# The first chunk of a two-FFN-and-attention kernel: seven up products lead its gates, the weight pieces are split in another order, and some small low parts move

## The chip, the cores and the metric

One core of a Trainium2 chip runs the whole program. The metric is device time in microseconds (us), from the start to the end of one execution. TensorE is called PE, VectorE DVE, ScalarE ACT, GpSimd POOL and SyncE SP, as in the profile; the SP engine issues most of the transfers.

## The reference

The input x has 2048 rows of 128 numbers. Three steps follow each other, each with a residual: half an FFN, attention, and the same half FFN again.

```
def ffn(x):                       # x: 2048 x 128, layer-normed
    shared = silu(x @ Ws_up) @ Ws_down              # 128 -> 64 -> 128
    aff = x @ centroids.T                           # 64 experts
    idx = top 8 of (aff + expert_biases)
    w = sigmoid(aff[idx]); w = w / (sum(w) + 1e-8)
    h = silu(x @ W_up[e]) for each of 64 experts    # 128 -> 64
    routed = sum_e cw[:, e] * (h_e @ W_down[e])     # cw: w scattered to 64 columns
    return shared + routed
x = x + 0.5 * ffn(layernorm(x))
x = x + softmax(q k^T) / sqrt(128) @ v              # q, k, v of layernorm(x)
x = x + 0.5 * ffn(layernorm(x))
```

All arrays are float32. All 64 experts are computed for every row, and the gates (cw) of the unchosen ones are zero.

## The kernel before, in words

**Chunks and units.** The rows are worked in chunks of 512 columns (the rows lie on the free axis, transposed). A chunk of the FFN has 33 units: unit 0 is the shared expert (64 partitions), and units 1 to 32 are pairs of experts (2 x 64 = 128 partitions). The FFN before the attention has chunks n = 0 to 3, that behind it n = 4 to 7. `U` is a unit's number counted over all chunks.

**Two parts for each product.** Every float32 operand of a product is split in a high part, rounded to float32r, and a low part, the rest. A product is then three matmuls: high by low, low by high, high by high (`product`, and the three lines of `down`, L1093 to L1095).

**One unit.** `up` (PE, L1055 to L1057) writes the hidden bank `hid[U % 4]`, one of four banks of PSUM. `silu_unit` (ACT, L430) applies silu. `gate_unit` (DVE, L672) multiplies by the gate row. `hi_unit` (ACT, L441) rounds the high part. `low_part` (L276) subtracts it, on DVE or, where `on_pool` says so, on POOL; in that case the gated value lies in one of three SBUF buffers `gated`, and else it lies in the hidden bank again. `down` (PE) adds the unit to `yacc`, four units behind `up`. `up` of unit U waits until bank U % 4 is free of unit U-4.

**Gates.** For units 7 to 32 a gate row comes by a transfer from DRAM, to which ACT's copy `gates` (L475) goes. For the units 1 to 6 of chunks 0 and 4 ("early" units) PE spreads the gate rows instead: `spread_gate` (L1080) multiplies the transposed weights `cwT` (ACT, L472) by a selection matrix, into one of two banks, so that unit u's spread waits for unit u-2's gate. Silu of an early unit writes into the SBUF buffer `wide`, and its gated value goes to the hidden bank.

**The order of the work** is written out by hand: each engine has its own program, with semaphores between them, and each works strictly in the order of its program. In the loop over units further steps hang on unit numbers: the prologue of the next chunk (its statistics, `normed` at units 5 and 6, PE's turn `pro_xT` at unit 8, L1134; `joint_product` at 11, `joint_turn` at 13, L1110, which waits for ACT's `joint_aff`, L450; the gate weights of the next chunk, POOL L374 and PE L1156 at 24).

**The first chunk's start.** ACT and DVE norm x, PE turns it (`first_xT`) and makes the affinities (`first_aff`); DVE picks the top 8 (`first_top`, `first_chosen`) and makes the weights (`first_weights`: L831, L832, L833). Meanwhile PE does `LEADS[0]` up products ahead, and `stay_awake` (L1223) matmuls whose result nobody reads. Then `pro_cw` (L1127) turns the weights, ACT copies them, and the loop over units begins. `LEADS` is (units of chunk 0, units of chunk 4).

**The weights.** W_up and W_down come in 8 pieces each of 128x512 numbers, into 14 buffers `raw`; even pieces are of W_up, odd ones of W_down, and one piece serves four units. `piece_hi` (ACT, L510) rounds a piece and `piece_lo` (POOL, L363) makes its low part. The first `PRE` pieces are split before the loop of chunk 0 and one more at each even unit. The semaphore `s_w` counts the split ones. `small` holds the small weights (centroids, Ws_up, Wv), `wsdn` the shared down weight, and `wsdn_pad` a padded copy that the shared expert of the chunks behind the first uses (`joint_down`). DVE's `small_lo` (L899) and `pad_lo` (L894) make their low parts; both subtract one SBUF tensor from another.

Of the kernel before, what the change touches and what calls it, by code (L numbers as in the profile page):

```python
# [35 lines left out]
PRE = 3  # L36
FIRST = 12
LEADS = (4, 2)
# [7 lines left out]
def macaron_kernel(nc, x_d, wup_d, wdn_d, wsup_d, wsdn_d, cent_d, bias_d, wq_d, wk_d, wv_d, gates_d, out_d):  # L46
# [21 lines left out]
    with ExitStack() as ctx:  # L68
# [178 lines left out]
        def on_pool(U):  # L247

            u, n = unit_at(U)
            if n == 0 and u < 25:  # L250
                return u > EARLY and u % 2 == 1
            return u == 15 or u % 3 != 0 and (u < UNITS - 1 or n % NCH < NCH - 1)
# [33 lines left out]
        def piece(k, part):  # L286

            w = (wup[part], flat(wdn[part]))[k % 2]
            return w[:, (k // 2) * PW:(k // 2 + 1) * PW]
# [4 lines left out]
        def _(sp):  # L294
# [8 lines left out]
            def load_piece(k):  # L303
                if k >= NR:
                    sp.wait_ge(s_w, k - NR + 1)
                src = (wup_d, wdn_d)[k % 2][:, (k // 2) * PW:(k // 2 + 1) * PW]
                sp.dma_start(raw[:, k % NR, :], src).then_inc(s_raw[k % NR], 16)

            for k in range(FIRST):
                load_piece(k)  # L310
                if k == 5:
                    load_x(1)
# [107 lines left out]
        def _(act):  # L420
            def silu_unit(u, n):
                U = place(u, n)
                m = P if u else F
                act.wait_ge(s_hid, U + 1)
                dst = hid[U % NH]
                if early_unit(u, n):
                    if nth_gated(u, n) > NB:
                        act.wait_ge(s_gated, nth_gated(u, n) - NB)
                    dst = wide[:, slot_of(u, n), :]
                nc.scalar.activation(dst[0:m, :], hid[U % NH][0:m, :], ACT.Silu).then_inc(s_silu, 1)  # L430
# [102 lines left out]
            for f in range(2):  # L533
                for c in range(NCH):
                    n = f * NCH + c
                    if c == 0:
                        if f == 0:
                            first_hi(0)
                            first_hi(1)
                            piece_hi(0)  # L540
                            act.wait_ge(s_value, 16 * 3)
                            nc.scalar.copy(small[0][:, E + F:LOADED], raws[:, E + F:LOADED]).then_inc(s_wh, 1)
                            nc.scalar.copy(wsdn[0][:, :], rawd[:, :]).then_inc(s_wh, 1)
                            act.wait_ge(s_spread, 1)
                            make_sel()
                            act.wait_ge(f_bias, 1)
                            nc.scalar.activation(flat(sil), bank[0][:, 0:TPC * E], ACT.Sigmoid).then_inc(p_sil, 1)
                            nc.scalar.activation(eps[:, 3:4], eps[:, 0:1], ACT.Silu)
                            piece_hi(1)
                            silu_unit(0, n)  # L550
                            silu_unit(1, n)
                            hi_unit(0, n)
                            silu_unit(2, n)
                            piece_hi(2)
                            pro_cwT(n)
                            silu_unit(3, n)
                    for u in range(min(c, 1), UNITS):
# [4 lines left out]
                        if n == 0 and u % 2 == 0 and PRE + u // 2 < 2 * WP:  # L562
                            piece_hi(PRE + u // 2)
                        if c + 1 < NCH:
                            if u == 9:
                                pro_hi(n + 1)
                            if u == 12:
                                joint_aff(n + 1)
                            if u == 13:
                                joint_silu(n + 1)  # L570
                            if u == 14:
                                joint_hi(n + 1)
                            if u == 16:
                                pro_sil(n + 1)
                            if u == 25:
                                pro_cwT(n + 1)
# [72 lines left out]
        def _(dve):  # L649
# [8 lines left out]
            def gate_unit(u, n):  # L658
# [3 lines left out]
                dve.wait_ge(s_silu, U + 1)  # L662
# [162 lines left out]
            def first_weights(n):  # L825
# [3 lines left out]
                inv = wsum[:, 1, :].unsqueeze(2).to_broadcast([P, TPC, E])  # L829
# [5 lines left out]
            def pro_sum(n):  # L835
# [4 lines left out]
                nc.vector.reciprocal(wsum[:, 1, :], wsum[:, 0, :]).then_inc(p_inv, 1)  # L840
# [45 lines left out]
            for f in range(2):  # L886
                for c in range(NCH):
                    n = f * NCH + c
                    if c == 0:
                        if f == 0:  # L890
# [18 lines left out]
                            small_lo(1, small, raws, E + F, LOADED)  # L909
                            small_lo(2, wsdn, rawd, 0, D)  # L910
                            lo_unit(0, n)
                            pad_lo()
                    for u in range(min(c, 1), UNITS):
# [3 lines left out]
                        if c + 1 < NCH:  # L917
                            if u == min(c, 1):
# [3 lines left out]
                            if u == 2:  # L922
                                stats(0, c + 1, p_st, (2, 3))
# [21 lines left out]
                        if c:  # L945
                            if u == 9:
                                epi_x(n - 1, c - 1)
                            if f == 0:
# [10 lines left out]
                                if u == 32:  # L959
                                    epi_proj_lo(c - 1)  # L960
                        if n == 0 and u == 14:
# [90 lines left out]
        def _(pe):  # L1052
# [6 lines left out]
            def up(u, n):  # L1059
                U = place(u, n)  # L1060
                if n == 0 and u and (u - 1) % (PAIRS // WP) == 0:
                    pe.wait_ge(s_w, 2 * ((u - 1) // (PAIRS // WP)) + 1)
                if U >= NH:
# [18 lines left out]
            def down(u, n):  # L1082
                U = place(u, n)
                m = P if u else F
                if n == 0 and u and (u - 1) % (PAIRS // WP) == 0:
                    pe.wait_ge(s_w, 2 * ((u - 1) // (PAIRS // WP)) + 2)
                if U == 0:
                    pe.wait_ge(s_wl, 3)
# [139 lines left out]
            for f in range(2):  # L1228
                for c in range(NCH):
                    n = f * NCH + c  # L1230
                    if n == 0:
# [5 lines left out]
                        stay_awake(2)  # L1237
# [167 lines left out]
```

## Time and profile before

| what | us |
|---|---|
| median of 3 runs (549.23 to 549.7) | 549.29 |
| the profiled execution | 549.5 |
| its span, first to last instruction | 547.7 |
| PE matmul busy | 533.3 (97%) |
| DVE / ACT / POOL busy | 408.5 / 412.2 / 274.6 |

The profile has one execution. The span is 1.8 us shorter than the time of the same execution. The program has no stage in which an engine other than PE is busy all the time for long; what is to be seen of the first chunk is where PE has gaps, and which engine's work ends last ahead of each.

### The profile page before, as it was taken

The page shows a single profiled execution, that of the slowest core. Times are in us where ns is not written, and L with a number is a line of the kernel's source. Part 1 is how long each engine was busy: PE and PEld are TensorE (multiplying, and loading weights), DVE is VectorE, ACT ScalarE, POOL GpSimd, SP SyncE. Part 2 cuts the span into 40 slices and gives each one's busy share as a digit, 9 for nine tenths or more (in the row PEclk, how much of TensorE's full clock was granted, in tenths as well). Part 3 has the DMA queues.
Part 4 walks back from the last instruction along what each step waited for, and adds up shares of the span by engine and source line. Part 5 has one row for each costly group of instructions (what it writes and reads, how often), then busy time and mean ns, then how long its engine had stood idle before and what let it go on. Part 6 is the DMA issues. An engine that isn't in the chain of part 4 may idle for free.

```text
span 547.7 us, 8638 instructions
## 1 busy us (share of the span) xinstructions
PE 533.3 (97%) x2683; PEld 436.2 (80%) x2683; DVE 408.5 (75%) x926; ACT 412.2 (75%) x814; POOL 274.6 (50%) x242
## 2 busy tenths in 40 slices
PE   8899999999999999899999998999999999999997
PEld 6677887887888886699999998877888888788885
DVE  5979679777966676667777888778677867966664
ACT  7899878877887775666666666678788777878774
POOL 3579767775866773000000000066675766766763
PEclk9999999999999999999999999999999999999999
DMA  8676554554565540000000000055565565656652
GB/s 259 189 203 198 182 193 164 178 194 154 173 187 181 187 156 1 1 1 1 1 2 0 2 1 1 11 183 162 176 197 174 177 185 178 175 170 193 198 192 95
DMA packets 44271, 72.25 MB, mean 132 GB/s; under 512 B 8865, under 2 KB 9633, under 8 KB 44225
## 3 DMA queue, kind: packets, MB, share of 16 engines
q1 hardware_dynamic: 43568, 71.17, 41.7%
q8 instruction: 21, 0.34, 0.3%
q10 hardware_dynamic: 592, 0.39, 0.2%
q0 software_dynamic: 64, 0.13, 0.1%
q14 instruction: 26, 0.20, 0.1%
HBM read 69.57 MB, written 2.10 MB: 131 GB/s over the span
## 4 chain that ended last, share of the span: by engine, by line
PE 87%; DVE 6%; ACT 3%; issue 2%; POOL 1%; POOLq 0%; DVEq 0%
PE lrow L1055 13%; PE lrow L1056 12%; PE lrow L1057 12%; PE bank L1093 10%; PE bank L1095 10%; PE bank L1094 10%; PE bank L1127 6%; PE bank L1327 3%; PE bank L1329 3%; PE bank L1328 3%; PE bank L1223 1%; POOL gpart_lo L276 1%; ACT gpart_hi L441 1%; DVE pmax L873 1%; PE bank L1134 1%
## 5 line engine op out<-in xcount | busy, mean ns | idle before, releaser
L276 POOL TENSOR_TENSOR gpart_lo<-gated,gpart_hi 128x512 fp32r<-128x512 f32 x174 | 224.5, 1296 | 168.3 <-ACT gpart_hi L441 163.9
L430 ACT ACTIVATE lrow<-lrow 128x512 f32<-128x512 f32 (+1 forms) x246 | 143.6, 584 | 64.7 <-PE lrow L1057 64.3
L672 DVE TENSOR_TENSOR gated<-lrow,wide 128x512 f32<-128x512 f32 x170 | 116.5, 685 | 51.2 <-ACT lrow L430 47.5
L441 ACT CAST gpart_hi<-gated 128x512 fp32r<-128x512 f32 x174 | 106.9, 614 | 2.9 <-DVE gated L672 2.5
L1093 PE MATMUL bank<-gpart_lo,wdn_hi 128*128 128x512 f32 x256 | 101.4, 396 | 1.0 <-POOL gpart_lo L276 1.0
L1095 PE MATMUL bank<-gpart_hi,wdn_hi 128*128 128x512 f32 x256 | 101.5, 396 | 0.0
L1094 PE MATMUL bank<-gpart_hi,wdn_lo 128*128 128x512 f32 x256 | 100.8, 394 | 0.0
L672 DVE TENSOR_TENSOR lrow<-lrow,wide 128x512 f32<-128x512 f32 x74 | 51.5, 697 | 34.9 <-ACT lrow L430 34.7
L990 DVE TENSOR_TENSOR pT_lo<-bank,pT_hi 128x512 fp32r<-128x512 f32 x64 | 43.7, 685 | 25.7 <-ACT pT_hi L616 25.7
L1093 PEld LDWEIGHTS bank<-gpart_lo,wdn_hi 128*128 128x128 f32 x256 | 48.0, 188 | 13.5 <-POOL gpart_lo L276 1.9
L276 DVE TENSOR_TENSOR gpart_lo<-lrow,gpart_hi 128x512 fp32r<-128x512 f32 (+1 forms) x84 | 57.3, 683 | 1.0 <-ACT gpart_hi L441 0.7
L609 ACT ACTIVATE prow<-lrow,nmax 128x512 f32<-128x512 f32 x64 | 44.4, 696 | 17.9 <-DVE nmax L878 17.9
L1095 PEld LDWEIGHTS bank<-gpart_hi,wdn_hi 128*128 128x128 f32 x256 | 48.1, 188 | 11.7
L1094 PEld LDWEIGHTS bank<-gpart_hi,wdn_lo 128*128 128x128 f32 x256 | 48.0, 188 | 11.3
L616 ACT CAST pT_hi<-bank 128x512 fp32r<-128x512 f32 x64 | 38.1, 595 | 24.9 <-PE bank L1127 24.8
L441 ACT CAST gpart_hi<-lrow 128x512 fp32r<-128x512 f32 (+1 forms) x84 | 49.8, 593 | 5.1 <-DVE lrow L672 4.9
L1055 PE MATMUL lrow<-xnT_lo_a,wup_hi 128*128 128x512 f32 x128 | 52.0, 406 | 0.1
L1055 PE MATMUL lrow<-xnT_lo_b,wup_hi 128*128 128x512 f32 x128 | 51.5, 403 | 0.0
L1056 PE MATMUL lrow<-xnT_hi_b,wup_lo 128*128 128x512 f32 x128 | 50.7, 396 | 0.0
L1057 PE MATMUL lrow<-xnT_hi_a,wup_hi 128*128 128x512 f32 x128 | 50.7, 396 | 0.0
L1056 PE MATMUL lrow<-xnT_hi_a,wup_lo 128*128 128x512 f32 x128 | 50.6, 395 | 0.0
L1057 PE MATMUL lrow<-xnT_hi_b,wup_hi 128*128 128x512 f32 x128 | 50.2, 392 | 0.0
(240 smaller groups left out, 946.0 us busy)
## 6 DMA issues: line engine op xcount, KB each, us to landing
wide<-gates_dram SPq DMA_DIRECT2D x488, 128.0 KB, 3.0
raw<-in_w_up SPq DMA_DIRECT2D x8, 256.0 KB, 5.6
raw<-in_w_down SPq DMA_DIRECT2D x8, 256.0 KB, 5.9
gates_dram<-gates SPq DMA_DIRECT2D x8, 128.0 KB, 2.3
x<-in_x SPq DMA_DIRECT2D x3, 256.0 KB, 4.3
out_dram<-x SPq DMA_DIRECT2D x3, 256.0 KB, 3.1
x<-in_x SPq DMA_DIRECT2D x1, 128.0 KB, 2.7
x<-in_x ACTq DMA_DIRECT2D x1, 128.0 KB, 2.9
```

Source lines behind the costliest of these rows:

```text
L276: return eng.tensor_tensor(gpart[1][0:m, U % NGP, :], gated_at(U)[0:m, :], gpart[0][0:m, U % NGP, :].bitcast(F32), ALU.subtract)
L430: nc.scalar.activation(dst[0:m, :], hid[U % NH][0:m, :], ACT.Silu).then_inc(s_silu, 1)
L441: nc.scalar.copy(gpart[0][0:m, U % NGP, :], gated_at(U)[0:m, :]).then_inc(s_ghi, 1)
L609: nc.scalar.activation(prow[:, j * CH:(j + 1) * CH], lrow[:, j * CH:(j + 1) * CH], ACT.Exp, bias=nmax[:, t % 2:t % 2 + 1], accum_out=psums ...
L672: nc.vector.tensor_tensor(gated_at(U), a, b, ALU.mult).then_inc(s_gated, 1)
L990: nc.vector.tensor_tensor(pT[1][at], tb[q % 2][:, :].rearrange("p (k n) -> p k n", n=P), pT[0][at].bitcast(F32), ALU.subtract).then_inc(a_ ...
L1055: nc.tensor.matmul(out, a[0], b[1], start=True, stop=False)
L1056: nc.tensor.matmul(out, a[1], b[0], start=False, stop=False)
L1057: return nc.tensor.matmul(out, a[0], b[0], start=False, stop=True)
L1093: nc.tensor.matmul(y, w[0], g[1], start=(U % (NCH * PAIRS + 1) == 0), stop=False)
L1094: nc.tensor.matmul(y, w[1], g[0], start=False, stop=False)
L1095: nc.tensor.matmul(y, w[0], g[0], start=False, stop=(u == UNITS - 1)).then_inc(s_down, 1)
```

## The change: seven leading up products, and another order of the small work

All of it is in the first chunk (n = 0).

- `LEADS[0]` goes from 4 to 7. The up products 4 to 6 wait only until silu of units 0 to 2 has left the bank (`s_silu`), since early units' silu writes to SBUF. Gates of units 1 and 2 write to banks 1 and 2, in which units 5 and 6 now stand, so they wait for silu of those.
- Unit 0 of chunk 0 goes to POOL's low parts (`on_pool`), and its silu to a `gated` buffer instead of the bank.
- ACT: pieces are split in the order 0, 2, 1, 3, 4 (`STEPS`), two of them ahead of the loop instead of three (`PRE`), the second ahead of the sigmoid; silus 0 to 4 come before the copies of the gate weights and silus 5 and 6 behind; the high part of unit 0 comes last. The high copy of the small Wv goes to unit 1.
- DVE: the statistics of chunk 1 move from units 1 and 2 to before the loop; the low part of small (Wv) and the padded copy move from there to unit 10; the reciprocal of the weights' sum is held in PSUM (`bank[0]`) instead of SBUF.
- SP: x of chunk 1 is loaded behind 2 pieces instead of 6, and the pieces in the new order.
- PE: one `stay_awake(2)` goes.

```diff
-PRE = 3
+PRE = 2
+STEPS = (0, 2, 1) + tuple(range(3, 16))
-LEADS = (4, 2)
+LEADS = (7, 2)
...
             if n == 0 and u < 25:
-                return u > EARLY and u % 2 == 1
+                return u == 0 or u > EARLY and u % 2 == 1
...
         def piece(k, part):
-            w = (wup[part], flat(wdn[part]))[k % 2]
-            return w[:, (k // 2) * PW:(k // 2 + 1) * PW]
+            i = STEPS[k]
+            w = (wup[part], flat(wdn[part]))[i % 2]
+            return w[:, (i // 2) * PW:(i // 2 + 1) * PW]
+        def split(i):
+            return STEPS.index(i) + 1
...
                 load_piece(k)
-                if k == 5:
+                if k == 1:
                     load_x(1)
...
-                dst = hid[U % NH]
+                dst = hid[U % NH] if U else gated_at(U)
...
                             act.wait_ge(s_value, 16 * 3)
-                            nc.scalar.copy(small[0][:, E + F:LOADED], ...).then_inc(s_wh, 1)
                             nc.scalar.copy(wsdn[0][:, :], rawd[:, :]).then_inc(s_wh, 1)
                             act.wait_ge(s_spread, 1)
                             make_sel()
+                            piece_hi(1)
                             act.wait_ge(f_bias, 1)
                             nc.scalar.activation(flat(sil), ..., ACT.Sigmoid).then_inc(p_sil, 1)
                             nc.scalar.activation(eps[:, 3:4], eps[:, 0:1], ACT.Silu)
-                            piece_hi(1)
-                            silu_unit(0, n)
-                            silu_unit(1, n)
+                            for u in range(5):
+                                silu_unit(u, n)
+                            pro_cwT(n)
+                            silu_unit(5, n)
+                            silu_unit(6, n)
                             hi_unit(0, n)
-                            silu_unit(2, n)
-                            piece_hi(2)
-                            pro_cwT(n)
-                            silu_unit(3, n)
...
+                        if n == 0 and u == 1:
+                            nc.scalar.copy(small[0][:, E + F:LOADED], ...).then_inc(s_wh, 1)
...
-                dve.wait_ge(s_silu, U + 1)
+                dve.wait_ge(s_silu, U + 1 + (NH if U + NH < LEADS[0] else 0))
...
-                inv = wsum[:, 1, :].unsqueeze(2)...
+                inv = (wsum[:, 1, :] if n else bank[0][:, TPC * (E + 1):TPC * (E + 2)]).unsqueeze(2)...
...
                             first_weights(n)
-                            small_lo(1, small, raws, E + F, LOADED)
-                            small_lo(2, wsdn, rawd, 0, D)
-                            lo_unit(0, n)
-                            pad_lo()
+                            small_lo(1, wsdn, rawd, 0, D)
+                            dve.wait_ge(s_x[1], 16)
+                            raw_stats(0, 1, (0, 1))
+                            stats(0, 1, p_st, (2, 3))
...
+                        if n == 0 and u == 10:
+                            pad_lo()
+                            small_lo(2, small, raws, E + F, LOADED)
...
         def up(u, n):
-                    pe.wait_ge(s_w, 2 * ((u - 1) // (PAIRS // WP)) + 1)
-                if U >= NH:
+                    pe.wait_ge(s_w, split(2 * ((u - 1) // (PAIRS // WP))))
+                if U >= NH and n == 0 and u < LEADS[0]:
+                    pe.wait_ge(s_silu, U - NH + 1)
+                elif U >= NH:
                     wait_hid_free(pe, U - NH)
...
         def down(u, n):
-                    pe.wait_ge(s_w, 2 * ((u - 1) // (PAIRS // WP)) + 2)
+                    pe.wait_ge(s_w, split(2 * ((u - 1) // (PAIRS // WP)) + 1))
                 if U == 0:
-                    pe.wait_ge(s_wl, 3)
+                    pe.wait_ge(s_wl, 2)
...
                         for u in range(LEADS[0]):
                             up(u, n)
-                        stay_awake(2)
                         pro_cw(n)
                         stay_awake(1)
```

## Rows read from the trace of the kernel before

**Rows 1.** The page, its first line.

```profile
span 547.7 us, 8638 instructions
```

**Rows 2.** Waits of PE between 26 and 160 us: us in total, times, longest.

```profile
PE bank L1156 <- POOL cw L374: 0.5, 1, 0.5
```

**Rows 3.** Windows: stretch, busy us per engine, granted clock (PEclk), DMA share, GB/s.

```profile
17.80:26.00 8.20, 7.60 (x30) 5.25 (x31) 8.00 (x24) 6.74 (x13) 5.58 (x6) 1.00 0.70 198
...
544.00:547.70 3.70, 0.63 (x4) 0.41 (x4) 0.75 (x2) 0.41 (x2) 0.00 (x0) 0.86 0.21 71
```

**Rows 4.** Timeline of PE: start us, us, line, tiles, count, idle before and releaser.

```profile
11.09 0.39 PE L1055 MATMUL lrow<-xnT_lo_a,wup_hi 128*128 128x512 f32 x1
...
11.79 1.03 PE L1223 MATMUL bank<-ident 128*128 128x256 f32 x4
...
14.15 0.66 PE L1127 MATMUL bank<-ident,cw 128*128 128x128 f32 x4 [1.33 <-DVE cw L833]
...
15.48 0.73 PE L1080 MATMUL bank<-cwT,sel 128*128 128x512 f32 x2 [0.24 <-ACT cwT L472]
...
17.23 0.49 PE L1080 MATMUL bank<-cwT,sel 128*128 128x512 f32 x1 [0.33 <-DVE lrow L672]
...
26.03 0.63 PE L1134 MATMUL bank<-ident,xn_a 128*128 128x128 f32 x4 [0.42 <-issue]
...
34.51 0.46 PE L1110 MATMUL bank<-ident,affT 64*128 64x64 f32 x4
```

**Rows 5.** Timeline of ACT, columns as in Rows 4.

```profile
9.69 0.39 ACT L547 ACTIVATE sil<-bank 128x256 f32<-128x256 f32 x1 [0.57 <-DVE biased_a L801]
...
11.50 0.61 ACT L510 CAST wdn_hi<-raw 128x512 fp32r<-128x512 f32 x1
...
12.01 0.58 ACT L430 ACTIVATE lrow<-lrow 64x512 f32<-64x512 f32 x1
...
14.84 0.59 ACT L472 CAST cwT<-bank 128x512 fp32r<-128x512 f32 x1 [0.28 <-PE bank L1127]
...
17.21 0.59 ACT L441 CAST gpart_hi<-lrow 128x512 fp32r<-128x512 f32 x1 [0.30 <-DVE lrow L672]
...
32.79 0.61 ACT L441 CAST gpart_hi<-gated 128x512 fp32r<-128x512 f32 x1
...
33.83 0.58 ACT L450 COPY affT<-bank 64x512 f32<-64x512 f32 x1
```

**Rows 6.** Timeline of DVE.

```profile
12.72 0.79 DVE L831 TENSOR_TENSOR rest<-rec,wsum 128x48 fp32r<-128x48 f32 x1
...
17.83 0.69 DVE L276 TENSOR_TENSOR gpart_lo<-lrow,gpart_hi 128x512 fp32r<-128x512 f32 x1
...
19.24 0.68 DVE L672 TENSOR_TENSOR lrow<-wide,bank 128x512 f32<-128x512 f32 x1
...
25.33 0.60 DVE L707 SCALAR_TENSOR_TENSOR xn_a<-x,mv,bank 128x128 f32<-128x128 f32 x2
...
31.25 0.69 DVE L672 TENSOR_TENSOR gated<-lrow,wide 128x512 f32<-128x512 f32 x1 [0.53 <-ACT lrow L430]
```

**Rows 7.** Line 831: ns min/median/max, first and last start, of its two executions.

```profile
L831 DVE TENSOR_TENSOR rest<-rec,wsum x2: 207/498/790, 12.7 to 347.3; 128x48 fp32r<-128x48 f32 x2
```

**Rows 8.** Timeline of POOL.

```profile
12.18 1.27 POOL L363 TENSOR_TENSOR wdn_lo<-raw,wdn_hi 128x512 fp32r<-128x512 f32 x1 [2.76 <-ACT wdn_hi L510]
...
19.65 0.22 POOL L358 TENSOR_SCALAR rs<-mv 128x4 f32<-128x4 f32 x1
...
19.96 1.04 POOL L359 TENSOR_TENSOR rs<-rs,mhalf 128x4 f32<-128x4 f32 x1
...
31.54 1.30 POOL L363 TENSOR_TENSOR wup_lo<-raw,wup_hi 128x512 fp32r<-128x512 f32 x1
```

**Rows 9.** Timeline of SP, its second weight piece.

```profile
3.15 0.43 SPq L307 DMA_DIRECT2D raw<-in_w_down  x1
```

**Rows 10.** DMA issues at 3.1 to 3.5: count, KB, median us to landing.

```profile
raw<-in_w_down SPq DMA_DIRECT2D x1, 256.0 KB, 5.0
```

More of the change, by code:

```diff
@@ L305, in load_piece @@
                     sp.wait_ge(s_w, k - NR + 1)
-                src = (wup_d, wdn_d)[k % 2][:, (k // 2) * PW:(k // 2 + 1) * PW]
+                i = STEPS[k]
+                src = (wup_d, wdn_d)[i % 2][:, (i // 2) * PW:(i // 2 + 1) * PW]
                 sp.dma_start(raw[:, k % NR, :], src).then_inc(s_raw[k % NR], 16)
@@ L541, in _ @@
                             act.wait_ge(s_value, 16 * 3)
-                            nc.scalar.copy(small[0][:, E + F:LOADED], raws[:, E + F:LOADED]).then_inc(s_wh, 1)
                             nc.scalar.copy(wsdn[0][:, :], rawd[:, :]).then_inc(s_wh, 1)
@@ L563, in _ @@
                             piece_hi(PRE + u // 2)
+                        if n == 0 and u == 1:
+                            nc.scalar.copy(small[0][:, E + F:LOADED], raws[:, E + F:LOADED]).then_inc(s_wh, 1)
                         if c + 1 < NCH:
@@ L828, in first_weights @@
                 dve.wait_ge(p_inv, n + 1)
-                inv = wsum[:, 1, :].unsqueeze(2).to_broadcast([P, TPC, E])
+                inv = (wsum[:, 1, :] if n else bank[0][:, TPC * (E + 1):TPC * (E + 2)]).unsqueeze(2).to_broadcast([P, TPC, E])
                 few = 2 * EARLY
@@ L839, in pro_sum @@
                 link(nc.vector.tensor_scalar(wsum[:, 0, :], total, 1e-8, None, ALU.add))
-                nc.vector.reciprocal(wsum[:, 1, :], wsum[:, 0, :]).then_inc(p_inv, 1)
+                nc.vector.reciprocal(wsum[:, 1, :] if n else bank[0][:, TPC * (E + 1):TPC * (E + 2)], wsum[:, 0, :]).then_inc(p_inv, 1)
             def epi_x(n, c):
@@ L917, in _ @@
                         if c + 1 < NCH:
-                            if u == min(c, 1):
+                            if n and u == min(c, 1):
                                 if f == 0:
@@ L921, in _ @@
                                 raw_stats(0, c + 1, (0, 1))
-                            if u == 2:
+                            if n and u == 2:
                                 stats(0, c + 1, p_st, (2, 3))
```

## The prediction

> **What bounds the kernel now.** I read the waits of PE first. Behind 26 us, and up to 160 us, the view lists one wait of 0.4 us that ends at 26.03 and one of 0.5 us behind POOL's L374, the gate weights of chunk 1 [rows 2, 4]. So PE runs without gaps from 26.03 to about 52, and what the change can move lies ahead of PE's turn at 26.03. PE's timeline shows the gaps there: 1.33 us before the turn of the gate weights at 14.15, filled only partly by L1223's idle matmuls from 11.79, then 0.24, 0.33 and some more up to 20, and 0.42 at 26.03 [rows 4]. The change puts three up products, real work, into the first gap.
>
> Then I asked what the turn at 26.03 waits for. The view says "issue", but it needs the normed tiles of chunk 1, and DVE's last two start at 25.33 and last 0.60, so they end at 25.93 [rows 6]. The window 17.8 to 26 has DVE busy 8.00 of 8.20 us, PE 7.60 [rows 3]. DVE is a closed chain there: low part of unit 1 at 17.83, gate 3 at 19.24, then gate, low part, gate, low part to the normed tiles [rows 6]. **So the end of this stage is set by DVE from 17.83 on, not by PE's work.** Whether PE did three products early or not matters only if DVE starts this chain earlier or has less in it.
>
> **The change, part by part.**
>
> *Leading ups (PE).* Ups 0 to 3 end their issue at 11.79; one up takes 11.79 - 11.09 = 0.70 [rows 4]. Up 4 now waits for silu 0. ACT's slot at 11.50, held by a piece's copy, is silu 0's now, because that copy goes ahead of the sigmoid [rows 5]. It lasts 0.58 and hands over in some 0.06 (cwT ends at 14.84 + 0.59 = 15.43, PE starts at 15.48 [rows 4, 5]): 12.14. Silu 1 and 2 follow every 0.5 us (12.01 - 11.50 [rows 5]), faster than an up, so ups 5 and 6 don't wait. Three ups take 2.10, and about 0.1 more for the first matmul after a gap (0.49 in the spread at 17.23 against 0.39 [rows 4]): PE is free at 14.34, where it was at the turn at 14.15. The turn is 0.19 later. The removed L1223 matmuls filled a gap and save nothing.
>
> *Gate weights (DVE).* L831 took 0.79 us while POOL ran a piece from 12.18 to 13.45, and 0.207 us in its other execution, at 347.3 [rows 6 to 8]. The new order ends that piece at about 10.8 (its high part is done at about 9.4), so the weights are ready 0.58 us sooner, at 13.5. PE comes at 14.34, so this is hidden: if PE were free it would be worth those 0.58 us.
>
> *A piece ahead of the sigmoid (ACT).* ACT idled 0.57 us before the sigmoid at 9.69 [rows 5]; a copy takes 0.5 of its time and the small copy that leaves gives 0.2. It fits if its piece has landed: issued at 3.15 [rows 9], with a landing time of 5.0 us [rows 10], 8.2 to 8.4, against a slot at 8.8. Cost 0; landing 0.5 later than that would begin to push the sigmoid.
>
> *ACT behind the turn.* cwT starts at 14.84 + 0.19 = 15.03 [rows 5]. Behind it come, at 0.49 each, cwT itself, the gates' copy, silu 5, silu 6, the high part of unit 0 and a piece: 2.94, and 0.20 for the small copy moved to unit 1. The high part of unit 1 starts at 18.17, where it was at 17.21 [rows 5]. It ends at 18.76, and DVE's low part of unit 1 starts at 18.82 instead of 17.83: 0.99 later. Gates 1 and 2 (behind silu 5 and 6 now) are done by 17.9 and don't hold it. Queued behind this low part is the whole DVE chain.
>
> *DVE's chain.* Between that low part and gate 3 lay 19.24 - 17.83 = 1.41 us [rows 6], 0.60 for the low part and 0.81 for chunk 1's statistics. These are now done ahead, in DVE's idle time from 14 to 16.6. So gate 3 starts at 18.82 + 0.60 = 19.42 against 19.24: **+0.18 us**. The padded copy and the low part of unit 0, which leave DVE as well, lay before the chain and shorten nothing in it.
>
> *POOL.* The high part of unit 0 ends at 17.6, then come its low part, pieces 2 and 3 at some 1.28 each: 21.4. The inverse deviation follows in 1.35 us (19.65 to 21.00 [rows 8]): 22.8. DVE wants it six steps of 0.60 behind gate 3, at 23.0. Hidden by 0.2; any excess passes on one for one. Shared down of unit 0 waits for POOL until 18.95; PE then has four downs, two ups and the rest up to the turn, about 6.1 us, and reaches it at about 25.1, where it waits for DVE until 26.21. The gap of 0.42 becomes about 1.1: **this is where the three early ups go.**
>
> *Transfers.* x of chunk 1 is issued some 2 us sooner, pieces 2 to 5 one slot later (0.5 us); all are used 4 us or more behind landing. Later pieces are split two units later than before; the nearest use (up 9 at 26.9, its piece split at about 24.1) has 2 us. No cost.
>
> *Unit 10 (DVE).* The padded copy and the small low part now stand between gate 10 and gate 11. Alone they take 0.2 to 0.3 each, and DVE idled 0.53 before gate 11 at 31.25 [rows 6]: cost 0. But both have two SBUF inputs, like L831, and POOL works without a break here until 31.54 + 1.30 = 32.84 [rows 8]. L831 shows that such a DVE instruction waits for the end of POOL's one [rows 6 to 8]. Upper bound: both wait for the end of the piece, gate 11 starts at 33.2 instead of 31.42, the high part of unit 11 at 33.9 instead of 32.97, and behind it on ACT stands L450 (33.83 [rows 5]), for which PE's turn at 34.51 waits [rows 4] with 0.1 to spare: PE stalls 0.9 us. Lower bound 0: DVE gets both done between two POOL instructions, at about 32.1, and ACT comes no later. I take 0, as no row shows DVE losing its turn to a second POOL instruction, and keep 0.9 for the range. The Trainium skill, SBUF — State Buffer, section "SBUF: two separate sides", says that a DVE operation with two SBUF inputs and a GpSimd one take the shared port pair for a whole instruction, whichever starts first, and the other fully blocks. By that rule with strict alternation the sum would have the 0.9. The trace agrees with the block itself (0.79 against 0.207 us) and has no case with two POOL instructions in a row.
>
> *The sum.* All behind 26.2 us is the same work in the same order, and up to 52 PE has no slack to give back; POOL's L374 shifts with DVE and ACT, so the 0.5 us wait stays. Span 547.7 + 0.2 [rows 1], with the 1.8 us around it 549.7, against this execution's 549.5, which is 0.2 above the median of 549.29. On the median: **549.5 us**.
>
> **Rivals.**
>
> *Unit 10 costs (slower side).* As above: 0.9 to 1.1 on top of 0.2, 550.4 to 550.6. Place: DVE at 30.8 to 33.2. It decides when POOL's next instruction starts before DVE's second one; from a gate 11 later than 32.3 on, each us is a us. For it: POOL's two instructions there follow each other without a gap. Against it: DVE's two also follow each other closely.
>
> *The lead pays (faster side).* If ACT reaches the high part of unit 1 as soon as gate 1 and 2 are done, 17.8, the removed statistics (0.81) shorten DVE's chain: up to -0.8, 548.5. Against it: six copies and silus at 0.49 behind cwT. PE's own bound is 25.1 instead of 26.03, so more than 1 us is not to be had.
>
> *The clock falls.* PE's only low grant in the rows is at the end, 0.86 with PE busy 0.63 of 3.70 us [rows 3]; elsewhere it is at 2.4 GHz. Afterwards PE has only the spread of unit 3 between about 16.3 and 18.95. Half clock in the 6.1 us of work behind it would cost up to 6.1 less the 1.1 of slack: +0.6 to +5, 550 to 554.5. Against it: gaps of 1.33 us didn't lower it.
>
> *POOL's inverse deviation is late.* +0.2 to +0.5 more, 549.7 to 550.
>
> **How the numbers follow.** The forecast, 549.3 to 549.8: 48%. Unit 10: 24%. The lead pays: 17%. Clock: 5%. POOL late: 6%. Within 0.2% (1.1 us, 548.2 to 550.4, what a measurement of this kernel tells from none) lies the forecast, the late POOL, most of the faster case and half of unit 10. Faster by more: 0.09. Slower: 0.19, from half of unit 10, the clock, and the ends of the others. Same: 0.72. The range 548.5 to 550.7 takes in both bounds of unit 10 and the full gain.
>
> **What would show it.** Ups 4 to 6 between 12.1 and 14.3; DVE's L831 at about 0.2 us; high part of unit 1 near 18.2; gate 3 near 19.4; a longer PE gap, about 1.1 us, ahead of L1134's turn, which starts at 26.2; at unit 10 the time of gate 11 (32.1 or 33.2) and whether PE stalls before L1110's turn. The prediction is wrong if the turn of chunk 1 comes before 25.8 or behind 26.6, or if PE does not wait ahead of it.

## The result, and the profile after

The changed kernel took 551.49 us (median of 8 executions, 550.47 to 552.35) against 549.36 for the kernel before (8 executions, 549.23 to 550.64): a ratio of 1.0028, with a 95% interval of 1.0017 to 1.0038. It is slower by 2.1 us, or 1.5 us by the ratio; the forecast was 549.5 with a range up to 550.7.

The profiled execution is the longest of the eight, 552.35 us with a span of 550.6 [rows 1: 547.7]. Its waits of PE up to 160 us:

```profile
...
PE bank L1105 <- POOL gpart_lo L277: 1.2, 1, 1.2
PE bank L1092 <- DVE lrow L679: 1.0, 1, 1.0
PE bank L1146 <- issue: 0.9, 1, 0.9
PE bank L1122 <- ACT affT L457: 0.8, 1, 0.8
PE bank L1220 <- DVE xn_a L794: 0.6, 1, 0.6
PE bank L1168 <- POOL cw L381: 0.5, 1, 0.5
```

The wait for POOL's gate weights is still 0.5 [rows 2]. Four are new or new in this size. L1122, the turn of the affinities, waits 0.8 for ACT's affT. L1220, PE's first turn of x at 6.66, waits 0.6. L1105 had been forecast, and like L1092 (the spread of unit 3's gate) it lies in slack ahead of the turn of chunk 1. PE's timeline:

```profile
11.48 0.63 PE L1065 MATMUL lrow<-xnT_lo_a,wup_hi 128*128 128x512 f32 x1
11.91 0.63 PE L1066 MATMUL lrow<-xnT_hi_a,wup_lo 128*128 128x512 f32 x1
...
16.23 0.60 PE L1139 MATMUL bank<-ident,cw 128*128 128x128 f32 x4
...
28.05 0.63 PE L1146 MATMUL bank<-ident,xn_a 128*128 128x128 f32 x4 [0.87 <-issue]
...
37.35 0.46 PE L1122 MATMUL bank<-ident,affT 64*128 64x64 f32 x4 [0.76 <-ACT affT L457]
```

The turn of the gate weights (L1139) is at 16.23 instead of 14.15, the turn of chunk 1 (L1146) at 28.05 instead of 26.03, and L1122 at 37.35 instead of 34.51 [rows 4]. So 2.02 us arise ahead of the turn of chunk 1 and 0.82 more between it and L1122: together 2.84 of the 2.9 by which the span grew. Behind that nothing is added. In the row at 11.48 a matmul of an up lasts 0.63 and the next starts 0.43 later, where an up had 0.70 for three in [rows 4]. The windows say why, granted clock in the column behind POOL:

```profile
9.00:12.00 3.00, 3.00 (x13) 2.40 (x13) 1.46 (x10) 2.19 (x4) 2.39 (x2) 0.54 1.06 404
12.00:15.00 3.00, 3.00 (x13) 2.44 (x12) 2.65 (x14) 2.85 (x6) 0.00 (x0) 0.89 0.98 360
...
18.00:21.00 3.00, 0.84 (x4) 0.33 (x3) 1.66 (x3) 3.00 (x7) 1.52 (x2) 1.00 0.21 44
21.00:24.00 3.00, 3.00 (x12) 1.89 (x13) 3.00 (x6) 2.29 (x5) 2.92 (x4) 1.00 0.71 215
```

So in this execution the clock was low at the head only; behind PE's gaps of 0.97 and 1.19 us, at 18 to 21 us, it stayed at 2.4 GHz.

ACT:

```profile
5.51 0.30 ACT L536 CAST small_hi<-raws 128x128 fp32r<-128x128 f32 x1 [0.98 <-DMA raws<-in_ws_up]
...
16.86 0.59 ACT L479 CAST cwT<-bank 128x512 fp32r<-128x512 f32 x1 [1.24 <-PE bank L1139]
...
20.01 0.59 ACT L448 CAST gpart_hi<-lrow 128x512 fp32r<-128x512 f32 x1
...
35.68 0.62 ACT L448 CAST gpart_hi<-gated 128x512 fp32r<-128x512 f32 x1 [0.78 <-DVE gated L679]
...
36.73 0.57 ACT L457 COPY affT<-bank 64x512 f32<-64x512 f32 x1
```

ACT waited for in_ws_up until 5.51 in this execution. Behind cwT, the high part of unit 1 (L448 at 20.01) stands 3.15 us, as forecast (18.17 - 15.03 = 3.14); affT ends at 37.30, and PE's turn starts at 37.35. DVE, and then POOL:

```profile
13.95 0.20 DVE L838 TENSOR_TENSOR rest<-rec,bank 128x48 fp32r<-128x48 f32 x1
...
14.52 0.21 DVE L840 TENSOR_TENSOR cw<-cw,rest 128x48 f32<-128x48 f32 x1
...
20.63 0.69 DVE L277 TENSOR_TENSOR gpart_lo<-lrow,gpart_hi 128x512 fp32r<-128x512 f32 x1 [0.89 <-ACT gpart_hi L448]
21.24 0.69 DVE L679 TENSOR_TENSOR lrow<-wide,bank 128x512 f32<-128x512 f32 x1
...
32.76 0.98 DVE L901 TENSOR_TENSOR wsdn_pad<-rawd,wsdn_hi 64x128 fp32r<-64x128 f32 x1
33.77 1.27 DVE L906 TENSOR_TENSOR small_lo<-raws,small_hi 128x128 fp32r<-128x128 f32 x1
34.97 0.68 DVE L679 TENSOR_TENSOR gated<-lrow,wide 128x512 f32<-128x512 f32 x1
```

```profile
32.30 1.29 POOL L277 TENSOR_TENSOR gpart_lo<-gated,gpart_hi 128x512 fp32r<-128x512 f32 x1 [0.47 <-ACT gpart_hi L448]
33.55 1.34 POOL L370 TENSOR_TENSOR wdn_lo<-raw,wdn_hi 128x512 fp32r<-128x512 f32 x1
```

L838 is at 0.20 us (L831's 0.79 in [rows 6]). POOL stood idle beside it, as its pieces ended at 11.49, so this doesn't show what the reciprocal in PSUM is worth by itself. The weights are ready at 14.73, and PE turns them at 16.23, 1.50 us later. Low part to gate 3 is 0.61 where it was 1.41 [rows 6]. At unit 10 the padded copy lasts 0.98 and the small low part 1.27; gate 11 starts at 34.97. The two DVE instructions alternate with POOL's: the first ends behind POOL's instruction of 32.30, the second behind the one of 33.55.

### The profile page after: what moved, and what is told of

Its sections match the earlier page's. It is cut to its first block, busy times and chain, and to the rows that moved or that the text cites. A ratio compares the mean times of both kernels' runs of the same rounds, so it can differ in the third digit from the quotient of the medians.

```text
span 550.6 us, 8630 instructions
## 1 busy us (share of the span) xinstructions
PE 533.9 (97%) x2679; PEld 436.3 (79%) x2679; DVE 408.0 (74%) x925; ACT 411.6 (75%) x814; POOL 275.4 (50%) x243
## 4 chain that ended last, share of the span: by engine, by line
PE 83%; DVE 6%; ACT 5%; issue 3%; POOL 1%; DMA 1%; POOLq 0%; SPq 0%; DVEq 0%; ACTq 0%
PE lrow L1065 12%; PE lrow L1066 12%; PE lrow L1067 12%; PE bank L1105 9%; PE bank L1107 9%; PE bank L1106 9%; PE bank L1139 6%; PE bank L1338 3%; PE bank L1339 3%; PE bank L1340 3%; ACT gpart_hi L448 1%; DVE gated L679 1%; POOL gpart_lo L277 1%; DVE pmax L880 1%; DVE gpart_lo L277 1%
## 5 line engine op out<-in xcount | busy, mean ns | idle before, releaser
L277 POOL TENSOR_TENSOR gpart_lo<-gated,gpart_hi 128x512 fp32r<-128x512 f32 (+1 forms) x175 | 225.5, 1294 | 176.0 <-ACT gpart_hi L448 171.5
L437 ACT ACTIVATE lrow<-lrow 128x512 f32<-128x512 f32 x245 | 143.0, 584 | 64.7 <-PE lrow L1067 64.2
L448 ACT CAST gpart_hi<-gated 128x512 fp32r<-128x512 f32 (+1 forms) x175 | 107.3, 613 | 3.6 <-DVE gated L679 3.3
L1105 PE MATMUL bank<-gpart_lo,wdn_hi 128*128 128x512 f32 x256 | 101.3, 396 | 1.0 <-POOL gpart_lo L277 1.0
L1105 PEld LDWEIGHTS bank<-gpart_lo,wdn_hi 128*128 128x128 f32 x256 | 48.0, 188 | 13.5 <-POOL gpart_lo L277 1.9
L277 DVE TENSOR_TENSOR gpart_lo<-lrow,gpart_hi 128x512 fp32r<-128x512 f32 x83 | 56.5, 681 | 1.8 <-ACT gpart_hi L448 1.5
L448 ACT CAST gpart_hi<-lrow 128x512 fp32r<-128x512 f32 x83 | 49.2, 592 | 5.4 <-DVE lrow L679 5.1
```

Source lines behind the costliest of these rows:

```text
L277: return eng.tensor_tensor(gpart[1][0:m, U % NGP, :], gated_at(U)[0:m, :], gpart[0][0:m, U % NGP, :].bitcast(F32), ALU.subtract)
L448: nc.scalar.copy(gpart[0][0:m, U % NGP, :], gated_at(U)[0:m, :]).then_inc(s_ghi, 1)
L1105: nc.tensor.matmul(y, w[0], g[1], start=(U % (NCH * PAIRS + 1) == 0), stop=False)
```

## Experiments

Twelve kernels ran in three groups, each group on one chip beside its own executions of the kernel before (medians 549.46, 549.76 and 549.60). "Ratio" is to those, with its 95% interval.

**The changed kernel again.**

> The changed kernel once more, unaltered. Theory A (the extra time has three parts: about 0.2 us from ACT's longer queue, 0.9 us from unit 10, and in some executions a head that is later and a TensorE clock that falls to half for one stretch between 9 and 21 us): times spread from 550.4 to 552.4 us, and the profiled execution shows either a full clock and a turn of chunk 1 (L1146) near 26.2 us, or a late turn together with a granted clock under 0.9 in some stretch of the first 21 us. Rival B (the later head is a fixed cost of the change): the turn is at 28 us again and ACT waits again 1 us for in_ws_up.

550.47 median, 550.32 to 554.39 in 12 executions; ratio 1.0025 [1.0014, 1.0037]. Ten of the twelve lie between 550.32 and 550.62. The profiled one has the small load in time, a weights' turn at 14.31, two gaps on PE of 0.97 and 1.19 us behind it, and a low clock between 20 and 24 us:

```profile
14.31 0.60 PE L1139 MATMUL bank<-ident,cw 128*128 128x128 f32 x4
...
17.29 0.49 PE L1092 MATMUL bank<-cwT,sel 128*128 128x512 f32 x1 [0.97 <-DVE lrow L679]
18.97 0.47 PE L1105 MATMUL bank<-gpart_lo,wsdn_hi 64*128 64x512 f32 x1 [1.19 <-POOL gpart_lo L277]
...
26.40 0.60 PE L1146 MATMUL bank<-ident,xn_a 128*128 128x128 f32 x4
```

and its windows:

```profile
19.00:20.00 1.00, 1.00 (x4) 0.58 (x4) 1.00 (x3) 0.69 (x2) 1.00 (x1) 1.00 0.54 170
...
21.00:22.00 1.00, 1.00 (x4) 0.71 (x4) 1.00 (x3) 0.74 (x2) 0.92 (x3) 0.50 0.74 254
```

ACT's first copy is at 4.42, without a wait for in_ws_up, and gate 11 and the turn of the affinities are at 33.09 and 35.47:

```profile
4.42 0.28 ACT L536 CAST small_hi<-raws 128x128 fp32r<-128x128 f32 x1
```

```profile
33.09 0.68 DVE L679 TENSOR_TENSOR gated<-lrow,wide 128x512 f32<-128x512 f32 x1
```

```profile
35.47 0.46 PE L1122 MATMUL bank<-ident,affT 64*128 64x64 f32 x4 [0.55 <-ACT affT L457]
```

So the steady part of the change is +1.0 us, and the late head is no fixed cost: rival B falls. Theory A holds for that, but not for the spread: of these twelve executions one alone is above 550.74, at 554.39.

**Nothing at unit 10.**

> The changed kernel, with the padded copy and the small low part taken from unit 10 back ahead of the loop (behind the statistics, where DVE is idle and POOL too), and the high copy of Wv back ahead of the sigmoid. Theory A: PE's wait before L1122 (0.8 us, on ACT's affT) is gone, and ACT reaches the high part of unit 1 0.2 us sooner: 0.9 to 1.1 us faster than the changed kernel under the same clock, so 549.4 to 551.3 us by the spread of the rest. Rival (unit 10 is hidden, the whole extra is clock and head): the same time as the changed kernel, the wait moves to the next step.

```diff
                             stats(0, 1, p_st, (2, 3))
+                            pad_lo()
+                            small_lo(2, small, raws, E + F, LOADED)
...
-                        if n == 0 and u == 10:
-                            pad_lo()
-                            small_lo(2, small, raws, E + F, LOADED)
```

(and ACT's high copy of Wv from unit 1 back ahead of the sigmoid.) 549.88 median, 549.49 to 551.55; ratio 1.0012 [1.0004, 1.0021]. PE's wait for affT is gone from the profile. The lowest execution is 0.83 us under the lowest of the changed kernel, the median 0.59. So unit 10 costs something, though the gain is smaller than the 0.9 to 1.1 expected. The low clock from 20 us on, which seven of the eleven executions probably have by their mean clock of 0.997 or less, may be the rest: it costs 0.26 us at the turn of chunk 1, and here no wait at unit 10 stands behind to hide it (see "Idle matmuls in the gaps").

**Unit 10 alone, on the kernel before.**

> The kernel before, with only the padded copy and the low part of Wv moved from ahead of the loop to unit 10. Theory A: each of the two waits for the end of a POOL instruction there (0.9 to 1.3 us instead of 0.2 to 0.3), gate 11 comes 1.9 us later, ACT's affT about 1.0 us and PE stalls some 0.9 us before the affinity turn; the loop's start gains nothing, as DVE's chain begins behind gates whose silu is there already, or up to 0.5 us, if the 0.94 us of the padded copy ahead of the statistics was what held gate 1. So +0.4 to +0.9 us: 549.8 to 550.3. Rival (hidden): 549.3 or up to 0.5 us faster.

549.92 median; ratio 1.0009 [1.0000, 1.0017], +0.46 us. Its waits of PE have the same new line, and its DVE the same pair:

```profile
PE bank L1111 <- ACT affT L450: 0.7, 1, 0.7
```

DVE at unit 10:

```profile
30.02 0.98 DVE L894 TENSOR_TENSOR wsdn_pad<-rawd,wsdn_hi 64x128 fp32r<-64x128 f32 x1
31.02 1.27 DVE L899 TENSOR_TENSOR small_lo<-raws,small_hi 128x128 fp32r<-128x128 f32 x1
```

The turn of chunk 1 came earlier, at 25.30 instead of 26.03 [rows 4]. Of these 0.73 us, 0.34 were there at the weights' turn already (13.81 instead of 14.15), before the edit could act; the other 0.39 are the padded copy, which no longer stood ahead of gate 1. From the turn of chunk 1 to that of the affinities it is 9.30 us (34.60 - 25.30) instead of 8.48. So the move is a loss of 0.8 and a gain of 0.4, which the median of +0.46 fits. No other edit stands in this run.

**Only the padded copy at unit 10.**

> The changed kernel with only the padded copy at unit 10; the small low part is ahead of the loop and the high copy of Wv ahead of the sigmoid. Theory A (the price of unit 10 is one POOL instruction for each of the two, and it decides only when gate 11 is later than ACT's own arrival): the one copy is done when POOL's current instruction ends, gate 11 starts 0.5 us later than in the kernel without it, PE's wait for affT is 0 to 0.2 us, and the time is that of the kernel with nothing at unit 10, 549.5 to 549.9 at the median. Rival (each blocked instruction costs PE its share): 0.4 us over that.

```diff
                         if n == 0 and u == 10:
                             pad_lo()
-                            small_lo(2, small, raws, E + F, LOADED)
```

(the small low part ahead of the loop, and ACT's high copy of Wv ahead of the sigmoid.) 550.17 median, 549.63 to 552.73, above the 549.5 to 549.9 expected; ratio 1.0016 [1.0006, 1.0026], which overlaps that of the kernel with nothing there, 1.0012. There is no wait for affT in its profile, and from the turn of chunk 1 (26.72) to that of the affinities (35.21) it is 8.49 us, as before.

```profile
31.44 0.98 DVE L900 TENSOR_TENSOR wsdn_pad<-rawd,wsdn_hi 64x128 fp32r<-64x128 f32 x1
32.46 0.69 DVE L678 TENSOR_TENSOR gated<-lrow,wide 128x512 f32<-128x512 f32 x1
```

and POOL:

```profile
30.99 1.29 POOL L277 TENSOR_TENSOR gpart_lo<-gated,gpart_hi 128x512 fp32r<-128x512 f32 x1 [0.48 <-ACT gpart_hi L448]
32.24 1.35 POOL L370 TENSOR_TENSOR wdn_lo<-raw,wdn_hi 128x512 fp32r<-128x512 f32 x1
```

One blocked instruction costs DVE 0.7 us and PE nothing; only the second makes ACT late. The POOL piece lasts 1.35 instead of 1.30: DVE's instruction went ahead of it.

**x of chunk 1 loaded late.**

> The changed kernel, with x of chunk 1 loaded behind 6 pieces as before. Theory C (the earlier x transfer delays the small loads at the head, in_ws_up above all, and so the clock falls): the late head goes, all executions at 550.4 to 550.7 us with in_ws_up landing at 4.5 us. Theory A (the late landing is chance, and the clock falls by PE's own gaps): the same spread as the changed kernel, 550.4 to 552.4 us.

```diff
-                if k == 1:
+                if k == 5:
                     load_x(1)
```

550.49 median, 550.41 to 553.21; ratio 1.0026 [1.0017, 1.0035]. The same times as the changed kernel beside it, so the early x costs nothing steady, and one execution at 553.21 shows that a long one doesn't need it. More can't be had from this run: the changed kernel itself had one long execution of twelve in this group, so whether the early x made the late heads of the first measurement more frequent isn't tested.

**Idle matmuls in the gaps.**

> The changed kernel, with idle matmuls into a free bank in PE's two gaps between 16.3 and 18.95 us (two calls of two each). Theory A: the granted clock stays at 2.4 GHz from 20 to 24 us, and the turn of chunk 1 comes 0 to 0.3 us sooner, because PE had about 1.1 us of slack ahead of it: time 550.1 to 550.5. Rival (the fall of the clock is what costs the 1 us): 549.4 to 549.7.

```diff
                             spread_gate(3, n)
+                            fill(2)
                             down(0, n)
...
+                        if n == 0 and u == 2:
+                            fill(2)
```

(`fill` is `stay_awake` into the bank of the gate copies, once they are read.) 550.49 median, 550.10 to 553.70; ratio 1.0023 [1.0010, 1.0035], no gain.

```profile
26.14 0.63 PE L1146 MATMUL bank<-ident,xn_a 128*128 128x128 f32 x4 [0.86 <-issue]
...
35.45 0.46 PE L1122 MATMUL bank<-ident,affT 64*128 64x64 f32 x4 [0.76 <-ACT affT L457]
```

and the windows:

```profile
18.00:21.00 3.00, 2.68 (x12) 1.58 (x10) 2.26 (x4) 2.64 (x7) 3.00 (x3) 1.00 0.41 136
21.00:24.00 3.00, 3.00 (x14) 2.21 (x13) 2.86 (x10) 2.30 (x5) 2.92 (x5) 1.00 0.83 243
```

The clock stays at 2.4 GHz, the turn of chunk 1 comes at 26.14 instead of 26.40, and PE waits 0.86 ahead of it. So the slack takes all but 0.26 us of the fall, and the wait at unit 10 takes the rest: the affinities are turned at 35.45 and 35.47. The mean clock of all executions agrees: 0.997 or less in eleven of the changed kernel's twelve, in one of eleven here, and the medians are alike.

What the fall needs is open. Seven profiles of the changed kernel and its variants have the same two gaps, 0.97 and 1.18 or 1.19 us. Three show the fall behind them (changed kernel again, x late, cold start), and four don't (changed kernel, nothing and one copy at unit 10, late load); in these four the small load was late.

**No warm start, in both kernels.**

> The kernel before, without the ten idle matmuls at the very start, so that TensorE is at 1.2 GHz when the affinities and the leading ups come. Theory A: the affinities are later by up to 1.4 us, but the four ups lie in the gap ahead of the weights' turn; the whole is 1.0 to 2.0 us slower than the kernel before.

> The changed kernel, without the ten idle matmuls at the start. Theory A (seven ups at half clock reach past the moment at which the weights are ready, so the changed kernel has lost the gap that hid a low clock): slower than the changed kernel by 1.0 to 2.0 us more than the kernel before loses by the same edit, 2.5 to 4 us in all. Rival (a low clock at the head costs both kernels the same, and its share in the slower executions is chance): both lose the same to within 0.3 us.

```diff
-WARM = 5
+WARM = 0
```

Before: 551.60 median of 6, ratio 1.0027 [1.0016, 1.0039]. Changed: 554.29 median of 4, ratio 1.0075 [1.0054, 1.0096]. The same edit costs the kernel before 1.8 us on its group's 549.76, and the changed one 3.8 us on the 550.47 of the first group. The profiled executions have their weights' turn at 16.14 and 16.52; the larger part arises behind it, where the changed kernel's clock was low from 21 to 27 us (0.50) and its turn of chunk 1 came at 29.72, against 27.56. So the expectation holds in size, while its reason, ups that reach past the weights, has only 0.2 us of it in these two (the turn of the weights is 2.21 later than in the changed kernel's second profile, and 1.99 later than in [rows 4]).

**A late small load, in three kernels.**

> The kernel before, with the biases loaded ahead of the centroids and in_ws_up, so that the small load for which ACT waits at the head is issued 0.47 us later in every execution. Theory A: ACT's first copies and with them the whole chain up to the turn of chunk 1 are 0.3 to 1.0 us later; PE's gap ahead of the weights' turn stays, and the time is 0.3 to 1.0 us over the kernel before.

> The changed kernel with the same reordering of the small loads. Theory A (the changed kernel has no gap left on PE in the first 16 us, so where the late head also lowers the clock its seven ups delay the weights' turn, and its gaps at 16 to 19 us bring a second fall): the same 0.3 to 1.0 us on its own floor of 550.4 where the clock stays, and 1.5 us and more where it falls between 9 and 13 us; the spread between its executions is larger than that of the kernel before with the same edit. Rival (a late head costs both the same): the same shift, the same spread.

> The kernel with four leads and the rest of the change, with the same reordering. Theory A: it behaves as the kernel before does, 0.3 to 1.0 us over its own 548.3, for its PE has a gap of about 0.8 us ahead of the weights' turn.

```diff
+            sp.dma_start(bias[:, :], bias_d.partition_broadcast(P)).then_inc(s_bias, 16)
             for src, lo, n in ((cent_d, 0, E), (wsup_d, E, F)):
                 sp.dma_start(raws[:, lo:lo + n], src).then_inc(s_small, 16)
-            sp.dma_start(bias[:, :], bias_d.partition_broadcast(P)).then_inc(s_bias, 16)
```

| kernel | median | lowest to highest | ratio |
|---|---|---|---|
| before, late load | 550.30 | 550.05 to 550.63 | 1.0012 [1.0003, 1.0021] |
| changed, late load | 552.93 | 551.15 to 553.63 | 1.0053 [1.0037, 1.0068] |
| four leads, late load | 548.93 | 548.75 to 549.42 | 0.9987 [0.9979, 0.9996] |

Issuing one load half a microsecond later costs the kernel before 0.7 us, the four-lead kernel 0.5 and the changed one 2.5 (the last two against their medians in the other groups; the changed kernel has four executions here). Theory A expected 0.3 to 1.0 for the kernel before and the four leads, and 1.5 and more for the changed kernel where the clock falls. In the profile of the changed kernel with it, PE, then DVE:

```profile
13.22 0.63 PE L1067 MATMUL lrow<-xnT_hi_a,wup_hi 128*128 128x512 f32 x1
13.65 0.60 PE L1065 MATMUL lrow<-xnT_lo_a,wup_hi 128*128 128x512 f32 x1
...
17.36 0.60 PE L1139 MATMUL bank<-ident,cw 128*128 128x128 f32 x4
```

```profile
15.41 0.21 DVE L840 TENSOR_TENSOR cw<-cw,rest 128x48 f32<-128x48 f32 x1
```

The weights are ready at 15.62 and turned at 17.36: they wait 1.74 us for the ups, whose first seven matmuls start some 0.43 us apart. In the kernel before with the late load it is PE that waits, and the weights lead:

```profile
14.64 0.65 PE L1127 MATMUL bank<-ident,cw 128*128 128x128 f32 x4 [1.34 <-DVE cw L833]
```

**Four leads, the rest of the change.**

> The changed kernel without its seven leading ups: four lead as before, unit 0's low part is on DVE again and its silu in the bank, ACT's order is silu 0, silu 1, high part 0, silu 2, silu 3, gate weights, and nothing stands at unit 10 (padded copy and small low part ahead of the loop). Kept are the early statistics, the piece split ahead of the sigmoid, the reciprocal in PSUM and the early x. Theory A (ACT's and DVE's queues set the turn of chunk 1, PE's early products are worth nothing): the weights are turned at about 13.6, the low part of unit 1 starts near 16.7, the turn of chunk 1 near 25.1 to 25.4 us, and the time is 0.6 to 1.0 us under the kernel before: 548.4 to 548.9. Rival (PE's products ahead are needed, as PE had 7.6 of 8.2 us busy there): the turn stays at 26.0 and the time at 549.2 to 549.5.

```diff
-LEADS = (7, 2)
+LEADS = (4, 2)
...
-                return u == 0 or u > EARLY and u % 2 == 1
+                return u > EARLY and u % 2 == 1
...
-                            for u in range(5):
-                                silu_unit(u, n)
-                            pro_cwT(n)
-                            silu_unit(5, n)
-                            silu_unit(6, n)
-                            hi_unit(0, n)
+                            silu_unit(0, n)
+                            silu_unit(1, n)
+                            hi_unit(0, n)
+                            silu_unit(2, n)
+                            silu_unit(3, n)
+                            pro_cwT(n)
```

(On DVE the padded copy, the small low part and the low part of unit 0 stand ahead of the statistics, ACT's high copy of Wv is ahead of the sigmoid, and PE's `stay_awake(2)` is back.) 548.47 median, 547.98 to 550.38; ratio 0.9978 [0.9968, 0.9987]. This beats both kernels. Its weights' turn and turn of chunk 1 on PE, then the low part of unit 1:

```profile
13.58 0.66 PE L1138 MATMUL bank<-ident,cw 128*128 128x128 f32 x4 [0.76 <-DVE cw L839]
...
24.82 0.63 PE L1145 MATMUL bank<-ident,xn_a 128*128 128x128 f32 x4
```

DVE:

```profile
17.40 0.69 DVE L277 TENSOR_TENSOR gpart_lo<-lrow,gpart_hi 128x512 fp32r<-128x512 f32 x1
18.01 0.69 DVE L678 TENSOR_TENSOR lrow<-wide,bank 128x512 f32<-128x512 f32 x1
```

The turn of chunk 1 is 1.21 us earlier than before [rows 4], with four ups ahead instead of seven. Of this 0.43 is the earlier start of DVE's chain (17.40 against 17.83), less than expected (16.7), and 0.80 are the statistics, which no longer stand in it (0.61 from the low part to gate 3, against 1.41 [rows 6]).

The kernel with nothing at unit 10 differs from this one by the three more ups, ACT's order, the engine of unit 0's low part and the place of some small steps, and has 1.0012 against 0.9978: 1.9 us. Which of these parts costs how much wasn't run.

## Why the prediction was wrong

**The frame held.** What sets the turn of chunk 1 is the chain ACT, then DVE. The steps of it came out where the small load was on time (the changed kernel's second profile): weights' turn 14.31 (14.34 forecast), and PE's gap ahead of the turn of chunk 1 at 0.86 and the turn at 26.14 (1.1 and 26.2) with the clock kept up. L838 took 0.20, the high part of unit 1 came 3.15 us behind cwT (3.14). The prediction's own sign of being wrong, a turn of chunk 1 behind 26.6, came in the first profile (28.05) and not in the second. Four leads with the rest of the change gain what the rival "the lead pays" said could be had from the removed statistics (0.8), and 0.4 by an earlier start of DVE's chain; but that kernel leads with four ups, as the kernel before does.

**Unit 10 was the first failed step: a term that was priced at 0 and costs 0.8.** Both bounds were in the text, and the upper one is what happened: gate 11 at 33.09 in the changed kernel's second profile (33.2), PE's wait for affT 0.5 to 0.8 (0.9). From the turn of chunk 1 to that of the affinities it is 8.48 us without the two copies [rows 4], and 9.30, 9.31 and 9.30 with them (first profile, idle matmuls, unit 10 alone). The ground for taking 0, that no row showed DVE losing its turn to a second POOL instruction, was no ground: the rows had no such case at all. DVE's two instructions and POOL's alternate in all seven profiles in which both stand there (0.96 to 0.98, and 1.27). The rule of the Trainium skill (SBUF — State Buffer, "SBUF: two separate sides"), that whoever starts first has the pair for its whole instruction, agrees with these rows; who is next it doesn't say, and the rows do. With the upper bound in the sum the forecast would have been 550.4, near the changed kernel's median in its second group, 550.47.

**The second failed step: "PE comes at 14.34, so this is hidden" took one execution's head for all.** The prediction gave the clock 5% and looked for it at the gaps behind 16 us. That fall occurs, costs 0.26 us at the turn of chunk 1 and nothing behind unit 10. What costs more comes ahead of it. In the first profile the small load was 0.9 us late (ACT's first copy at 5.51; 4.60 in the profile of the kernel before, 4.42 in the second one), PE had a gap of 0.59 ahead of its first turn, and from about 9.2 to 12.6 us the clock was at 1.2 GHz. The kernel before has 1.33 us of PE gap ahead of the weights' turn [rows 4], which can take up ups that come at a low clock. The three early ups fill just this gap, so each 0.2 us per matmul goes straight to the weights' turn: the weights waited 1.50 us for the ups in the first profile, and 1.74 with the late load. With the load made late by 0.47 us, the price was 2.5 us against 0.7, and with four leads 0.5. Of the ten executions of the kernel before with the late load two had a mean granted clock of 0.997, and took 550.32 and 550.63 (median 550.30). If their clock was low at the head, which no profile shows, the gap took most of it up. PE has no longer gap in [rows 4] than this one.

The 551.49 of the first measurement is then 0.8 from unit 10, 0.1 from the longer ACT queue (a turn of chunk 1 at 26.14 instead of 26.03; 0.18 forecast), and, in five of eight executions, 0.8 to 1.9 more. The longest of the five was profiled, and has it at the head; for the other four that is argued. Why more executions had the late head in that group than in the second is open. A late load alone is not enough: in the profiles of the kernels with nothing, and with one copy, at unit 10, ACT waited 0.82 and 0.88 us for the load (0.98 in the first profile), the 512-column matmuls kept their 0.23 us spacing, and the turn of chunk 1 came at 26.66 and 26.72, 0.5 to 0.6 late. That the late load brings the clock down through PE's gap at 6 us is argued, not shown, and the gap's length alone doesn't decide: it is 0.59 and 0.55 us in the two profiles with the fall, and 1.08, 0.92 and 0.93 in three without it (nothing and one copy at unit 10, and the kernel before with the late load). Open is also what makes a small load late by 0.9 us, and how the price of the late head divides between fewer gaps on PE early and the second fall of the clock: the late-load profile has only the first, the cold-start one mostly the second.

## What to carry to other kernels

Real work in a gap of the fastest engine earns nothing if the serial chain behind the gap doesn't start sooner, and it takes away the slack that absorbs a late transfer or a low clock; look for the queue that starts the chain, and shorten that. Two VectorE instructions with two SBUF inputs each, put where GpSimd works without a break, wait for one GpSimd instruction each (0.98 and 1.27 us here instead of 0.3); one may be free where two are not. A term whose bounds are 0 and 0.9 us isn't to be set to 0 because the trace lacks an example of the worst case.

## What the runs showed of the hardware

- A DVE instruction that waits goes ahead of POOL's next one (POOL's piece 1.35 instead of 1.30 us), and DVE's next one, although queued directly behind, waits for that POOL instruction (1.27 instead of 0.29): strict alternation.
- The granted clock fell to 0.50 from about 20 to 23.5 us behind two PE gaps of 0.97 and 1.19 us, with the spread of one unit between them, in the changed kernel's second profile; the same two gaps did not do it in its first, nor gaps of 1.33 and 0.24 in the kernel before. Four idle matmuls in the gaps kept it up in ten of eleven executions. In the Trainium skill, TensorE: Matmul & The Clock Gate, the section "HAM oscillation — how this bites in real kernels" describes bursts of matmuls that start at half clock behind waits; here the waits ahead of the fall were for DVE and POOL, and not for a transfer.
- In the late-load profile of the changed kernel the granted clock is given as 1.00 throughout the head, while matmuls of 512 columns start 0.43 us apart, as they did at a granted 0.54. It is the same in both profiles with the cold start. At the start of an execution the spacing tells the clock, not the column.
